# The query projection of a group's first head moved from its second slot to its first, in layers 1 and 4

## What is computed

```python
x = x + jnp.tanh(g_xattn[0]) * _L0_xattn_ref(_layernorm(x, axis=-1), ctx_4096, ...)
...
q = (query @ Wq + bq).reshape(B, L, NKV, G, HDIM)
k_, v_ = jnp.split(kv @ Wkv + bkv, 2, axis=-1)
...
scores = jnp.einsum('blkgd,bmkd->bkglm', q, k) * scale
attn = jax.nn.softmax(scores, axis=-1)
o = jnp.einsum('bkglm,bmkd->blkgd', attn, v).reshape(B, L, NHEAD * HDIM)
return o @ Wo + bo
```

## Time and profile before

| | |
|---|---|
| median of 3 runs | 2156.29 us (2155.64 to 2157.31) |
| profiled execution, own time | 2155.29 us |
| its span, first to last instruction | 2153.5 us |
| matmul engine busy | 1971.2 us, 92% |
| VectorE busy | 1475.5 us, 69% |
| ScalarE busy | 1029.6 us, 48% |
| GpSimd busy | 938.5 us, 44% |
| matmul engine waits for pT_lo (L909) | 34.1 us in 37 waits |
| matmul engine waits for ScalarE's exponential (L1085) | 18.7 us in 11 waits |

### The profile page before, as it was taken

How to read it: one execution, slowest core, us unless ns; L and a number is a source line. 1 busy time by engine, 2 the same in 40 slices (tenths; PEclk the granted TensorE clock), 3 DMA queues, 4 the chain that set the end, 5 groups by cost and what they waited for, 6 DMA issues and landing times.

```text
span 2153.5 us, 33307 instructions
## 1 busy us (share of the span) xinstructions
PE 1971.2 (92%) x10874; PEld 1651.7 (77%) x10874; DVE 1475.5 (69%) x2725; ACT 1029.6 (48%) x2264; POOL 938.5 (44%) x971
## 2 busy tenths in 40 slices
PE   5999999999748999998988999997799999999997
PEld 4788888888636888887666888886678888888886
DVE  5777787777777887887334555656467766677676
ACT  3666666666514544553123544542155555545552
POOL 2555554554445665664321323322144444444432
PEclk9999999999978999999988999999899999999999
DMA  3222221122211111111210101001101110111001
GB/s 140 57 64 75 77 85 57 61 74 67 92 34 40 63 65 54 52 45 64 67 54 4 34 8 34 23 1 55 54 11 47 47 46 11 50 45 45 14 23 45
DMA packets 47070, 106.77 MB, mean 50 GB/s; under 512 B 6065, under 2 KB 21937, under 8 KB 43105
## 3 DMA queue, kind: packets, MB, share of 16 engines
q1 hardware_dynamic: 46944, 105.14, 15.3%
HBM read 98.37 MB, written 6.75 MB: 49 GB/s over the span
## 4 chain that ended last, share of the span: by engine, by line
PE 64%; DVE 18%; ACT 9%; issue 7%; POOL 1%; DVEq 0%; ACTq 0%; POOLq 0%
PE psX L369 23%; PE psQ L369 11%; PE psS L369 11%; PE psO L369 10%; PE psT L752 5%; DVE pT_lo L909 2%; ACT pT_hi L1092 1%; DVE dq_space L461 1%; DVE nmax L897 1%; ACT dq_space L448 1%; DVE p_sb L891 1%; DVE nbias L895 1%; PE psT L369 1%; ACT p_sb L1085 1%; DVE qscr L470 1%
## 5 line engine op out<-in xcount | busy, mean ns | idle before, releaser
L1202 POOL TENSOR_SCALAR p_sb<-p_sb,rrec 128x512 f32<-128x512 f32 (+1 forms) x320 | 266.0, 831 | 704.1 <-DVE rrec L905 704.0
L1092 ACT ACTIVATE pT_hi<-psT 128x512 fp32r<-128x512 f32 (+2 forms) x384 | 235.0, 612 | 336.9 <-PE psT L752 336.0
L909 DVE TENSOR_TENSOR pT_lo<-psT,pT_hi 128x512 fp32r<-128x512 f32 (+2 forms) x384 | 271.4, 707 | 81.9 <-ACT pT_hi L1092 81.9
L369 PE MATMUL psO<-pT_hi,v_hi 128*128 128x256 f32 (+1 forms) x832 | 255.1, 307 | 41.0 <-DVE pT_lo L909 34.1
L752 PE MATMUL psT<-ident,p_sb 128*128 128x128 f32 x1600 | 243.3, 277 | 13.9 <-POOL p_sb L1202 10.5
L369 PE MATMUL psO<-pT_hi,v_lo 128*128 128x256 f32 (+1 forms) x832 | 237.0, 285 | 0.0
L369 PE MATMUL psO<-pT_lo,v_hi 128*128 128x256 f32 (+1 forms) x832 | 237.0, 285 | 0.0
L752 PEld LDWEIGHTS psT<-ident,p_sb 128*128 128x128 f32 x1600 | 195.9, 142 | 53.1 <-POOL p_sb L1202 15.8
L369 PE MATMUL psQ<-xnT_hi,wq_hi 128*128 128x512 f32 (+1 forms) x448 | 189.0, 422 | 18.7 <-DVE qscr L869 9.2
L1085 ACT ACTIVATE p_sb<-psS,nbias 128x512 f32<-128x512 f32 (+1 forms) x192 | 145.3, 757 | 126.6 <-DVE nbias L899 126.6
L369 PEld LDWEIGHTS psO<-pT_hi,v_hi 128*128 128x128 f32 (+1 forms) x832 | 155.0, 186 | 54.2 <-DVE pT_lo L909 45.9
(11 more groups left out here) (337 smaller groups left out, 4786.2 us busy)
## 6 DMA issues: line engine op xcount, KB each, us to landing
wq_f<-in_a_wq SPq DMA_DIRECT2D x96, 256.0 KB, 2.7
wo_f<-in_a_wo SPq DMA_DIRECT2D x24, 1024.0 KB, 6.1
wkv_f<-in_a_wkv SPq DMA_DIRECT2D x24, 512.0 KB, 3.9
mask_sb<-in_codes SPq DMA_DIRECT2D x32, 174.0 KB, 2.4
qscr<-in_amax SPq DMA_DIRECT2D x32, 174.0 KB, 2.3
w<-qscr SPq DMA_DIRECT2D x32, 174.0 KB, 1.9
wo_f<-in_f_wT SPq DMA_DIRECT2D x3, 1024.0 KB, 5.2
wq_f<-in_a_wq SPq DMA_DIRECT2D x16, 192.0 KB, 2.3
```

What stands on the lines that cost most here:

```text
L369: mm = pe.matmul(dst, w, m, start=(first and k == 0), stop=(last and k == n - 1))
L909: L.t_lo.inc(dve.tensor_tensor(pT_view(L, pT_lo, j), t_view(L, j), pT_view(L, pT_hi, j).bitcast(F32), ALU.subtract))
L1092: L.t_hi.inc(act.activation(pT_view(L, pT_hi, j), t_view(L, j), ACT.Copy))
L1202: L.s_norm.inc(pool.tensor_scalar(p_view(L, j), p_view(L, j), rrec[:, j:j + 1], 1.0, ALU.mult, ALU.mult))
```

## The change

In `Layer.__init__` a second table of slots, `q_pe`, is made from `q_slot`. It is the same, except that in layers 1 and 4 its entry for head 0 is 0 in place of 1. Only the matmul engine's `head` reads it. ScalarE, VectorE and GpSimd still split the query of that projection in slot 0.1.

```diff
         self.kt, self.q_slot, self.settle = self.keys // P, cfg["q_slot"], cfg["settle"]
+        self.q_pe = (0,) + self.q_slot[1:] if cfg["q_slot"] == (1, 1, 1, 3) else self.q_slot
...
                     if j == L.slots // 2:
                         weighted_v(g, h, 0)
-                    if j == L.q_slot[h] and L.head(g, h, L.q_lead):
+                    if j == L.q_pe[h] and L.head(g, h, L.q_lead):
                         q_proj(*L.head(g, h, L.q_lead))
```

## The result

| | before | after |
|---|---|---|
| median | 2156.29 us (2155.01 to 2158.45, 7 runs) | 2163.75 us (2161.17 to 2165.56, 7 runs) |
| ratio | | 1.0032, 95% interval 1.0020 to 1.0044 |
| profiled execution, own time (span) | 2155.29 us (2153.5) | 2161.88 us (2160.1) |
| matmul engine busy | 1971.2 us | 1978.4 us |
| mean granted clock | 0.968 | 0.964 |

The kernel is 0.32% slower, and the changed kernel taken once more gave 1.0026 (1.0016 to 1.0037). (A ratio stands with its interval; the quotient of the two medians can differ from it by up to 0.0004.) The forecast was +4.45 us; the medians differ by 7.5 and 5.3 us, the profiled executions by 6.6. Three of the seven executions lie above that end.

A forecast was written before the change was run, and what follows sets the result against it. The matmul engine was taken as the bound, with 64% of the chain of waits. Bank wait 1.4, later scores 0, first groups of layers 1 and 4 1.2 and 1.85: 2156.29 + 4.45 = 2160.7 us, range 2157.0 to 2163.8.

The forecast's parts named there:

- that end: Whole kernel's time: the upper end of the predicted range, 2163.8 us.

The follow-up runs named there:

- e2: The kernel before with the move in layer 4 alone, layer 1 as before: 2158.12 us, ratio 1.0007.
- e12: The changed kernel once more, unaltered, against the kernel before: 2162.56 us, ratio 1.0026.
- e11: The kernel before with one move in layer 4's first group, the small unit of slot 0.0 behind the scores of slot 0.1: 2159.50 us, ratio 1.0016.

## What to carry to other kernels

Put a matmul step that needs a bank where the bank has been free for longer than a weight load's lead, and take the delay from semaphore to weight load from a row of the same kind of wait. When a stretch in which work changes contains or adjoins a low granted clock, price it twice, with the stretch kept and with it moved or shortened, and look at every other such stretch behind it too. In a kernel whose unchanged executions differ by 0.35%, as here, a difference of two medians of 0.2% says little on the order of the work; the delay from one projection to the next, profile against profile, told 0.28 to 0.31 us a group of layer 1 in every kernel that had the wait.

## What the runs showed of the hardware

- The same instructions at the same place ran at 1.00 or 0.50 depending on the execution (50.6 to 54.1 in before and e2). In two profiles of one kernel (after, e12) the same last 64 us differ by 4.0 us, and in all fourteen they go by where the first stretch at 0.50 falls in the program (2112.9, 2120.2 or 2121.3 in before's time).
- The low clock can pin a program: the delay into layer 1's first group shrank from 1.28 to 0.85 us, because the clock rose at 68.9 and 69.1 whatever the program had done by then.
- Which matmuls the engine executes after it has resumed changes when the clock rises: 2.8 to 2.9 us later (transposes, then projection; seven profiles), 6.1 to 6.3 (transposes, small unit, then scores or projection; six), 9.7 (transposes, scores, small unit; e11 alone).
- The restart of a matmul stream costs 0.08 us beyond its wait, and the first weight load behind a wait for q_lo came 0.12 to 0.13 us after the releasing VectorE instruction's end in all 14 groups of after, against 0.05 behind the wait for pT_lo.
